# Expert tiles of 128 rows, four to a unit, in place of two of 256

## The reference

```python
x = x + 0.5 * ffn(layernorm(x))
x = x + attention(layernorm(x))     # per sequence; softplus(gelu(..)) features, 16 heads of 16
x = x + 0.5 * ffn(layernorm(x))

# ffn: per token 4 of 16 experts, from sigmoid scores within the best 2 of 4 groups
g = einsum('th,eih->tei', x, gate_w); u = einsum('th,eih->tei', x, up_w)    # i = 128
yo = einsum('tei,ehi->teh', silu(g) * u, down_w)
routed = einsum('te,teh->th', combine, yo)      # combine: normalised top-4 weights x 2.5
return routed + shared_mlp(x)                   # two more experts that every token visits
```

## Time and profile before

| | us |
|---|---|
| median of 3 runs | 1950.2 |
| lowest and highest run | 1946.7, 1955.36 |
| the profiled execution | 1945.92 |
| its span, first to last instruction | 1944.2 |
| TensorE busy | 1629.1 |
| POOL busy | 1115.1 |
| VectorE busy | 1031.3 |
| ScalarE busy | 923.8 |

### The profile page before, as it was taken

The page is one execution under the profiler, slowest core; times in us unless marked ns, Lnnn a source line. Parts: engine busy times, 40 slices in busy tenths (PEclk is TensorE's granted clock), DMA queues, the critical chain, the costliest instruction groups (busy, mean ns, idle before and its releaser), DMA issues.

```text
span 1944.2 us, 36213 instructions
## 1 busy us (share of the span) xinstructions
PE 1629.1 (84%) x11159; PEld 1253.8 (64%) x11159; DVE 1031.3 (53%) x3186; ACT 923.8 (48%) x1435; POOL 1115.1 (57%) x1249
## 2 busy tenths in 40 slices
PE   5679999979989999999999999996999998887100
PEld 4447776757777777777777777774777676665100
DVE  4775747634455456557547456556646655232323
ACT  5334443424666556565665656654656642232000
POOL 2677757777033644554454564465466677454676
PEclk9889999999999999999999999999999999999555
DMA  9839998999646855775785785663598799999453
GB/s 311 323 133 249 262 246 245 257 252 258 156 112 168 211 139 146 199 202 146 196 197 153 173 216 155 168 188 87 123 240 212 200 258 289 254 259 296 133 164 118
DMA packets 586145, 393.48 MB, mean 202 GB/s; under 512 B 396375, under 2 KB 547054, under 8 KB 585966
## 3 DMA queue, kind: packets, MB, share of 16 engines
q1 hardware_dynamic: 536626, 256.85, 53.6%
q0 software_dynamic: 49152, 134.28, 22.7%
q10 hardware_dynamic: 188, 0.03, 0.0%
HBM read 101.61 MB, written 197.13 MB: 154 GB/s over the span
## 4 chain that ended last, share of the span: by engine, by line
PE 47%; POOL 20%; DVE 11%; issue 10%; SPq 5%; DMA 5%; ACT 3%; POOLq 0%; DVEq 0%; ACTq 0%
POOL xd L1320 11%; PE bank L993 10%; POOL yg L1334 8%; PE bank L848 6%; PE bank L850 6%; PE bank L849 6%; PE bank L1035 5%; SPq L829 3%; PE bank L997 3%; DVE xb L1547 2%; DMA yg<-yd,idx 2%; DMA xtp<-xd 2%; PE bank L1096 2%; PE bank L937 2%; PE bank L938 2%
## 5 line engine op out<-in xcount | busy, mean ns | idle before, releaser
L1320 POOL DMA_INDIRECT xd<-xs,idx x512 | 517.5, 1011 | 421.9 <-DVE picked L1471 216.4
L1334 POOL DMA_INDIRECT yg<-yd,idx x512 | 505.7, 988 | 231.4 <-issue 152.3
L993 PE MATMUL bank<-dn,h 128*128 x1408 | 377.6, 392 | 57.8 <-ACT ybuf L1190 26.9
L848 PE MATMUL bank<-xtp,gu_hi 128*128 128x256 f16 x1408 | 387.4, 275 | 28.9 <-DMA xtp<-xd 13.5
L1190 ACT ACTIVATE ybuf<-bank 128x512 f32<-128x512 f32 x352 | 209.5, 595 | 389.8 <-PE bank L993 381.4
L849 PE MATMUL bank<-xtp,gu_hi 128*128 128x256 f16 x1408 | 387.0, 275 | 0.0
L850 PE MATMUL bank<-xtp,gu_lo 128*128 128x256 f16 x1408 | 386.8, 275 | 0.0
L1522 DVE SCALAR_TENSOR_TENSOR h<-bank,h 128x512 f32<-128x512 f32 x240 | 165.6, 690 | 321.5 <-PE bank L850 265.5
L993 PEld LDWEIGHTS bank<-dn,h 128*128 128x128 f32 x1408 | 251.3, 194 | 111.5 <-issue 77.9
L1547 DVE SCALAR_TENSOR_TENSOR xb<-yg,comb,xb 128x256 f32<-128x256 f32 x512 | 208.2, 478 | 164.7 <-DMA yg<-yd,idx 164.6
L1183 ACT ACTIVATE h<-bank 128x512 f32<-128x512 f32 x240 | 141.6, 595 | 215.0 <-PE bank L850 126.3
(11 more groups left out here) (191 smaller groups left out, 2527.5 us busy)
## 6 DMA issues: line engine op xcount, KB each, us to landing
yd<-ybuf SPq DMA_DIRECT2D x352, 256.0 KB
xr<-xb SPq DMA_DIRECT2D x32, 512.0 KB, 4.7
xb<-xr SPq DMA_DIRECT2D x32, 512.0 KB
xd<-yg SPq DMA_DIRECT2D x3, 4096.0 KB, 14.6
xb<-in_attn_x_dram SPq DMA_DIRECT2D x16, 512.0 KB
xd<-xs,idx POOLq DMA_INDIRECT x512
yg<-yd,idx POOLq DMA_INDIRECT x512
out_dram<-xb SPq DMA_DIRECT2D x16, 512.0 KB, 3.3
```

The source lines that it names most:

```text
L848: pe.matmul(out_ap, a_hi, b_hi, start=(i == 0), stop=False)
L993: last = pe.matmul(dst, h[:, g % RING_H, c], w, start=True, stop=True)
L1320: pool.indirect_dma_start(out=xd[q % NC][:, :], out_offset=bass.IndirectOffsetOnAxis(ap=idx[:, r % SEQS, t, k:k + 1], axis=0), in_=xs[:, r ...
L1334: pool.indirect_dma_start(out=yg[:, half, t % 2, j].bitcast(U32), out_offset=None, in_=yd[q % NC][:, :], in_offset=bass.IndirectOffsetOnAx ...
```

## The change

`SLOT` becomes 128. A stage has fewer padded rows: 79 tiles of 128 instead of 48 of 256, rounded up to whole units. A unit still has 512 rows, but four tiles with an expert each. The planner goes on counting in half units of 256 rows (`tiles`: 40 or 56 a stage, 304 in all); the small tiles are 608 and the units 152, where there were 176. `SHARE` (2) is the number of small tiles in a half unit. For a unit there are now four transposing DMAs of 128 rows, four stores of 128 rows, gate and up matmuls of 128 columns, twice as many, and four down products with an expert each. The zeroing of the pads halves. The table counts an expert's tiles in two halves of 16 steps. The planner's costs of some pieces change, and with them the order on all engines.

```diff
-SLOT = 256
+SLOT = 128
+SHARE = TOK // SLOT // 2
...
-            tiles = (n * TOK * TOPK + E * (SLOT - 1)) // SLOT
-            tiles += tiles % 2
+            tiles = -(-(n * TOK * TOPK + E * (SLOT - 1)) // SLOT // (2 * SHARE)) * 2
...
-        SP=dict(wload=0.5, load=0.5, store=0.5, zero_rows=1.0, xload=2.6, ystore=0.5),
+        SP=dict(wload=0.5, load=0.5, store=0.5, zero_rows=1.0, xload=3.6, ystore=0.9),
...
-                for a in range(2):
-                    row_of[2 * p + a] = found[a]
+                for a in range(2 * SHARE):
+                    row_of[2 * SHARE * p + a] = found[a]
                     sp.dma_start(xtp[:, p % RING_P, :, a * SLOT:(a + 1) * SLOT], xd[q % NC][bass.ds(found[a], SLOT), :],
                                  transpose=True).then_inc(xp_loaded[p % RING_P], 16)
...
-                sp.dma_start(yd[q % NC][bass.ds(row_of.pop(t), SLOT), :].rearrange("(j p) c -> p j c", j=2),
-                             ybuf[:, t % RING_Y].bitcast(U32)).then_inc(y_stored[t % RING_Y], 16)
+                for j in range(SHARE):
+                    sp.dma_start(yd[q % NC][bass.ds(row_of.pop(SHARE * t + j), SLOT), :],
+                                 ybuf[:, t % RING_Y, j].bitcast(U32)).then_inc(y_stored[t % RING_Y], 16)
...
-                for a in range(2):
+                for a in range(2 * SHARE):
                     e = expert_of[i][a]
                     c = slice(a * SLOT, (a + 1) * SLOT)
                     xp = xtp[:, i % RING_P, :, c]
-                    if m and a:
+                    if m and a == 2 * SHARE - 1:
                         find_next(g)
...
-                        e = expert_of[i][b]
-                        c = slice(b * SLOT + j * P, b * SLOT + (j + 1) * P)
+                        e = expert_of[i][SHARE * b + j]
+                        c = slice((SHARE * b + j) * P, (SHARE * b + j + 1) * P)
...
+                link(5, dve.tensor_scalar(held[:], held[:], -float(E * SLOT), None, ALU.add))
+                link(6, dve.tensor_tensor(fills, held[:].unsqueeze(2).broadcast_to([P, E, E]),
+                                          slot_steps[:].unsqueeze(1).broadcast_to([P, E, E]), ALU.is_gt))
+                link(7, dve.tensor_reduce(n_more[:], fills, AX_X, ALU.add))
+                link(8, dve.tensor_tensor(n_of[:], n_of[:], n_more[:], ALU.add))
```

More of the change, by code:

```diff
@@ L56 @@
 MIX_STEPS = 4
-TABLE_STEPS = 14
+TABLE_STEPS = 18
 CONSTS = 29
@@ L80 @@
     WEIGHT = dict(
-        SP=dict(wload=0.5, load=0.5, store=0.5, zero_rows=1.0, xload=2.6, ystore=0.5),
-        PE=dict(turn_w=0.5, small=0.4, turnR=0.95, logits=0.75, rank=0.25, turn_tab=0.3, gate=1.36, up=1.36, down=0.89,
+        SP=dict(wload=0.5, load=0.5, store=0.5, zero_rows=1.0, xload=3.6, ystore=0.9),
+        PE=dict(turn_w=0.5, small=0.4, turnR=0.95, logits=0.75, rank=0.25, turn_tab=0.3, gate=1.5, up=1.5, down=0.89,
                 turnA=0.95, proj=2.65, second=3.5, gproj=1.36, kv=1.85, z=0.5, apply=1.85, regroup=0.95, out=4.4),
@@ L90 @@
                  kv_mask=0.45, mix=3.0, gate_out=1.45, residual=1.4))
-    MOVES = dict(wload=0.8, load=1.6, store=1.6, zero_rows=11.0, xload=3.2, ystore=0.85, scatter=1.7, gather=1.7)
+    MOVES = dict(wload=0.8, load=1.6, store=1.6, zero_rows=5.5, xload=3.2, ystore=0.85, scatter=1.7, gather=1.7)
     TABLE = dict(sigmoid=("exp", "gelu", "silu"), silu=("silu",), gelu=("gelu",), gate_gelu=("gelu",), exp=("exp",), ln=("ln",))
@@ L526, in macaron @@
         n_of = sb("n_of", [P, E])
+        n_more = sb("n_more", [P, E])
         upto_n = sb("upto_n", [P, E])
@@ L533, in macaron @@
         t_cols = sb("t_cols", [P, 2])
-        tiles_max = max(st["tiles"] for st in stage)
+        tiles_max = SHARE * max(st["tiles"] for st in stage)
         tab = sb("tab", [P, NC, 2, tiles_max], I32)
@@ L742, in tab_of @@
             q = plan.stage_of_tile(2 * p)
-            i = 2 * p - stage[q]["tile"]
-            return tab[0:1, q % NC, column, i:i + 2]
+            i = SHARE * (2 * p - stage[q]["tile"])
+            return tab[0:1, q % NC, column, i:i + 2 * SHARE]
         def shared_over(r):
@@ L804, in zero_rows @@
             def zero_rows(i):
-                block_of_zeros = yg[:, 0, 0].rearrange("p k d -> p (k d)").bitcast(F16)[:, 0:2 * ROW]
+                block_of_zeros = yg[:, 0, 0].rearrange("p k d -> p (k d)").bitcast(F16)[:, 0:ROW]
                 if i == 0:
@@ L809, in zero_rows @@
                 pads = xd[i][:, :].rearrange("(e r) c -> e r c", e=E)[:, 0:SLOT, :]
-                sp.dma_start(pads.rearrange("e (p j) c -> p e (j c)", j=2),
-                             block_of_zeros.unsqueeze(1).broadcast_to([P, E, 2 * ROW])).then_inc(spare_zeroed[i], 16)
+                sp.dma_start(pads.rearrange("e p c -> p e c"),
+                             block_of_zeros.unsqueeze(1).broadcast_to([P, E, ROW])).then_inc(spare_zeroed[i], 16)
             row_of = {}
@@ L963, in gate_ @@
                         find_experts(i)
-                    pe.wait_ge(xp_loaded[i % RING_P], 32 * (i // RING_P + 1))
+                    pe.wait_ge(xp_loaded[i % RING_P], 32 * SHARE * (i // RING_P + 1))
                     if i == 0:
@@ L1497, in table_cols @@
                 link(4, dve.tensor_reduce(n_of[:], fills, AX_X, ALU.add))
-                link(5, dve.tensor_tensor(fills, n_of[:].unsqueeze(1).broadcast_to([P, E, E]), upto[:], ALU.mult))
-                link(6, dve.tensor_reduce(upto_n[:], fills, AX_X, ALU.add))
+                link(5, dve.tensor_scalar(held[:], held[:], -float(E * SLOT), None, ALU.add))
+                link(6, dve.tensor_tensor(fills, held[:].unsqueeze(2).broadcast_to([P, E, E]),
+                                          slot_steps[:].unsqueeze(1).broadcast_to([P, E, E]), ALU.is_gt))
@@ L1500, in table_cols @@
+                link(7, dve.tensor_reduce(n_more[:], fills, AX_X, ALU.add))
+                link(8, dve.tensor_tensor(n_of[:], n_of[:], n_more[:], ALU.add))
+                link(9, dve.tensor_tensor(fills, n_of[:].unsqueeze(1).broadcast_to([P, E, E]), upto[:], ALU.mult))
+                link(10, dve.tensor_reduce(upto_n[:], fills, AX_X, ALU.add))
                 dve.scalar_tensor_tensor(out=first_row[:], in0=upto_n[:], scalar=-float(SLOT), in1=base[:], op0=ALU.mult, op1=ALU.add)
                 dve.tensor_scalar(dead_row[:], tile_no[:], upto_n[:, E - 1:E], region, ALU.subtract, ALU.mult)
-                link(7, dve.tensor_scalar(ended[:], upto_n[:], tile_no[:, 0:1], None, ALU.is_le))
+                link(11, dve.tensor_scalar(ended[:], upto_n[:], tile_no[:, 0:1], None, ALU.is_le))
@@ L1503, in table_cols @@
                 dve.tensor_scalar(live[:], ended[:, E - 1:E], -1.0, 1.0, ALU.mult, ALU.add)
-                link(8, dve.tensor_reduce(t_expert[:], ended[:], AX_X, ALU.add))
+                link(12, dve.tensor_reduce(t_expert[:], ended[:], AX_X, ALU.add))
                 dve.tensor_scalar(t_cols[:, 0:1], t_expert[:], float(E - 1), None, ALU.min)
-                link(9, dve.tensor_scalar(of_tile[:], expert[:], t_expert[:, 0:1], None, ALU.is_equal))
-                link(10, dve.tensor_tensor(of_tile[:], of_tile[:], first_row[:], ALU.mult))
@@ L1508, in table_cols @@
-                link(11, dve.tensor_reduce(t_first[:], of_tile[:], AX_X, ALU.add))
-                link(12, dve.tensor_scalar(t_first[:], t_first[:], tile_row[:, 0:1], -1.0, ALU.add, ALU.add))
-                link(13, dve.tensor_tensor(t_first[:], t_first[:], dead_row[:], ALU.subtract))
-                link(14, dve.scalar_tensor_tensor(out=t_cols[:, 1:2], in0=t_first[:], scalar=live[:, 0:1], in1=dead_row[:],
+                link(13, dve.tensor_scalar(of_tile[:], expert[:], t_expert[:, 0:1], None, ALU.is_equal))
@@ new lines, in table_cols @@
+                link(14, dve.tensor_tensor(of_tile[:], of_tile[:], first_row[:], ALU.mult))
+                link(15, dve.tensor_reduce(t_first[:], of_tile[:], AX_X, ALU.add))
+                link(16, dve.tensor_scalar(t_first[:], t_first[:], tile_row[:, 0:1], -1.0, ALU.add, ALU.add))
+                link(17, dve.tensor_tensor(t_first[:], t_first[:], dead_row[:], ALU.subtract))
+                link(18, dve.scalar_tensor_tensor(out=t_cols[:, 1:2], in0=t_first[:], scalar=live[:, 0:1], in1=dead_row[:],
```

4 lines of the change are left out of this document (2 added, 2 removed).

## The result

The changed kernel takes 2028.35 us in the median (2028.13 to 2029.92) against 1951.39 for the kernel before: a ratio of 1.0404, interval 1.0369 to 1.0438. It is 77 us slower, where the forecast was 1922 us and the range ended at 2000.

The account below looks back on a forecast made before the run. TensorE was taken to bound the middle, SyncE the last stage, POOL the tail and first stage. Terms -18 - 5 + 13 - 21 + 5 = -26 from 1945.9 us gave 1920, adjusted to 1922 us; range 1865 to 2000.

Parts of the forecast that it names:

- A load of 128 rows: SyncE's time T for a transposing load of 128 rows: taken as 0.80 us, between ends of 0.61 and 1.30.
- The rival of a price per instruction: SyncE's 128-row transposing load takes 1.30 us; 53 us lost in the last stage, 17 in the first; 1977 us; chance 0.15.
- The last stage, +13: 1650 to 1810 us, paced by SyncE: 20 units of 8.21 us against 24 of 6.29, 13 us lost.
- 5.01 + 4T: SyncE's time in us for a last-stage unit after the change, T being one transposing load of 128 rows: 8.21 us.
- Where SyncE is free: Outside the last stage, SyncE's two more stores a unit hide behind waits for TensorE; nothing counted.
- TensorE's middle, -18: 365 to 1310 us: fewer units save 47 us of array time, sequencer exposure takes 29, so 18 us gained.
- the exposure of 0.34 us a unit: TensorE's sequencer, slowed by register work for narrower matmuls, ends 0.34 us a unit short; 29 us over 84 units.
- The rival of attention's chain: Latencies, not TensorE's work, pace the middle, so gains of 18 and 5 us do not come; 1943 us; chance 0.14.
- 1400 to 1650 us, -5: 27.6 units become about 24.2: TensorE's array saves 13 us, sequencer exposure takes 8, so 5 us gained.
- The tail, -21: After the last product, one sequence of 16 POOL gathers goes, 21 us less.
- The table, +5: Four more VectorE steps in each of six tables of tiles: between nothing and 10 us, counted as 5 us lost.
- Lost leads: TensorE's sequencer waits for products and exposes 1.1 us a unit; middle 45 us slower; 2002 us; chance 0.14.

Follow-up runs that it names:

- b_loads4: Kernel before with each transposing load of 256 rows cut into two of 128, four a unit, all else unchanged: 2038.05 us, ratio 1.0442.
- b_thin: Kernel before with only one of the three matmuls in each group of the routed gate and up: 1906.11 us, ratio 0.9762.
- b_seq128b: Kernel before with 128-column gate and up matmuls, register work for each doubled group, expert numbers in a table of their own: 2018.08 us, ratio 1.0343.
- b_fewer40: Kernel before, tiles of 256 rows kept, with only as many units as the changed kernel has: 1876.96 us, ratio 0.9627.
- a_static: Changed kernel with each tile's expert fixed in the program, so no register work or load of experts on TensorE: 2009.63 us, ratio 1.0298.
- a_both_costs: Changed kernel with two transposing loads of 256 rows a unit, fixed experts and planner costs that fit: 1889.16 us, ratio 0.9686.
- a_costs: Changed kernel with the planner's costs of before, which changes the order alone: 2010.81 us, ratio 1.0297.
- b_seq128: Kernel before with 128-column gate and up matmuls, register work for each doubled group, each expert number read twice: 2154.94 us, ratio 1.1036.
- b_loads1: Kernel before with one transposing load of 512 rows a unit in place of two of 256: 1986.08 us, ratio 1.0193.

## Why the prediction was wrong

- **A load of 128 rows (failed).** "So I take 0.37 us as the part that stays and halve the other 0.86: T = 0.80 us, nearest the lower end." It takes 1.19 us. I carried a plain load's behaviour over to a transposing one; no row showed that the 0.86 us go with rows, and the time lies near the upper end of 1.30. The rival of a price per instruction, at 0.15, had the mechanism, but not the sizes: it put 53 us into the last stage and 17 into the first, where 18 and 31 came.
- **The last stage, +13.** It came out near (160 to 178 us from first load to last store), for wrong reasons: T was 0.4 us too short, but of the 1.38 us of stalls that I kept 0.5 are left (0.36 + 4 x 1.33 + 4 x 0.47 = 7.6 of 8.1 us), at a DMA share of 0.85 in place of 1.06, and the load of row numbers fell from 0.99 to 0.36 us. 5.01 + 4T with T = 1.19 would have given 9.8 us a unit; it is 8.1.
- **Where SyncE is free (failed).** "SyncE's two more stores a unit are behind waits for TensorE elsewhere" and nothing for the first stage: b_loads4 shows 31 us before the first attention's result, 24 of them by the first stage's last store, and the chains of after show SyncE in the first and the second stage. The mean of 11 us a unit in the middle said nothing of the stages in which units come faster.
- **TensorE's middle, -18 (failed).** The array saved 44 us in the ten sequences (670 to 626, by the sum used for b_thin), where 68 units became 58 and the forecast's prices give 40; the exposure of 0.34 us a unit is 0.35 there (28 us on 68 units in b_seq128b, less 0.06 of array). Both sizes were right. What failed is that they add up to a gain: waits grew from 37 to 86 us. A second limit stands 3% behind TensorE, of which POOL's scatters and gathers are a part. Work taken off TensorE shows little (19 of 117 us in b_thin, 16 of 38 in b_fewer40), work put on it shows (28 us in b_seq128b). 16 us of gain against 28 x 58 / 68 = 24 of price give +8, and +6 was measured; since fixed experts take 10 us back (a_static) and not 24, how the 22 us above b_fewer40 divide stays open. The busy share of 97% said which engine led, not by how much. The rival of attention's chain, at 0.14, was right that little comes, but POOL stands in that limit too.
- **1400 to 1650 us, -5 (failed).** The five sequences take 30 us more. Static experts take 14 of them back (365 us; it is 379 here), two loads 4, the old costs 7 (372), all three together 20 (a_both_costs, 359). What decides between them stays open.
- **The planner (no term).** Its new costs took 18 us. That the order moves with the costs stood in the change; I counted it at nothing without a row for it.
- **The tail, -21.** Right: 135 to 113 us, by one sequence of gathers that lies ahead of the last store. The full size came with this order: with the same units b_fewer40 gains 10, and so does a_costs.
- **The table, +5.** No run tells it apart.
- **Lost leads, at 0.14.** Not what happened in the middle: 0.41 us a unit, where 1.1 was its price. In the stretch to the last store b_seq128b loses 0.9 us a unit, near that price, where neither the sum nor this rival had a term for TensorE; in the changed kernel, where SyncE is late, fixed experts take 3 us off it (a_static).

## What to carry to other kernels

Bound an instruction whose duration no row shows by the nearest row of the same kind, and keep its full price until a row shows that it scales. Before counting a gain on the engine that leads, find how far behind it the next limit stands: leave out much of its work in one run and see how little comes off. And an experiment that doubles a cost must be read for the cost it brings along, as the load of numbers in b_seq128 showed.

## What the hardware showed that I had not expected

- A transposing load's issue hardly depends on its rows up to 256: 1.19 us for 128 (after, b_loads4), 1.25 for 256 (before, whole span) in the medians; for 512 it is 1.57 at least and 2.29 in the median (b_loads1).
- A TENSOR_LOAD of four neighbouring numbers is quicker than one of two: on TensorE 0.333 us in the median in the row below, against 0.558, and two numbers read twice each took 1.22 us.

```profile
L921 PEldq TENSOR_LOAD <-tab x152: 327/333/1023, 153.1 to 1898.7; - x152
```

- Moving the stores to another engine's queue made the kernel 4.5% slower, although it took the stores from the queue that the chain of waits named. What ScalarE's own waits cost in it was not separated.
